# Patch embedding of a vision tower in nine full tiles of 128 patches, moved into attention tiles by transfers

## What is computed

```python
patches = _patchify(x, PATCH)                               # 32 x 36 x 768
tokens = jnp.einsum('bnd,ed->bne', patches, W) + b
out = jnp.concatenate([cls, tokens], axis=1)
h = out + pos_embedding
...
h = jnp.concatenate([jnp.broadcast_to(cls_tok, ...), h], axis=1)   # 32 x 38 x 256
h = h + _L0_attn_ref(_layernorm(h), ...)     # 1 + s + s*s/2, causal, divided by the row's sum
h = h + _L0_ffn_ref(_layernorm(h), ...)      # values and weights rounded to a 4-bit grid
h = h + _L1_attn_ref(_layernorm(h), ...)     # softmax, causal
h = h + _L1_ffn_ref(_layernorm(h), ...)      # gelu between low-rank products
```

## Time and profile before

| | |
|---|---|
| median of 3 runs | 257.46 us (257.4 to 257.49) |
| profiled execution | 258.99 us, its span 257.3 us |
| TensorE busy | 238.8 us (93%), 3077 records |
| VectorE busy | 183.2 us (71%) |
| ScalarE, GpSimd busy | 144.1 us (56%), 153.4 us (60%) |
| mean granted clock of TensorE | 0.996 |

### The profile page before, as it was taken

One profiled execution on the slowest core, in us unless ns is written; L12 is line 12 of the kernel. 1 busy time (PEld: TensorE's weight loads), 2 busy tenths in 40 slices (PEclk: granted clock), 3 DMA queues, 4 the chain that ended last, 5 costly groups with the idle time before them and its releaser, 6 DMA issues.

```text
span 257.3 us, 7730 instructions
## 1 busy us (share of the span) xinstructions
PE 238.8 (93%) x3077; PEld 187.0 (73%) x3077; DVE 183.2 (71%) x348; ACT 144.1 (56%) x322; POOL 153.4 (60%) x234
## 2 busy tenths in 40 slices
PE   6599999979999799999999998899999998989992
PEld 6488888858888687887887887688888885344331
DVE  0434968324679999999999999998768888377021
ACT  3122314287998677878746754574555556823640
POOL 6432888525966777795889749676656661155000
PEclk9999999999999999999999999999999999999998
DMA  5959942000000000000001010001101110001021
GB/s 149 242 135 248 302 103 65 0 0 4 3 3 3 0 3 3 3 0 4 4 20 36 25 40 29 20 30 40 35 28 34 33 35 33 3 0 54 19 75 48
DMA packets 12967, 12.26 MB, mean 48 GB/s; under 512 B 4464, under 2 KB 12356, under 8 KB 12932
## 3 DMA queue, kind: packets, MB, share of 16 engines
q1 hardware_dynamic: 12504, 11.76, 16.8%
q10 hardware_dynamic: 428, 0.01, 0.1%
HBM read 7.95 MB, written 1.25 MB: 36 GB/s over the span
## 4 chain that ended last, share of the span: by engine, by line
PE 61%; DVE 27%; issue 5%; DMA 3%; ACT 2%; SPq 0%; DVEq 0%; ACTq 0%
PE psum L1329 11%; PE psum L1398 9%; PE psum L1567 4%; DVE img L1092 4%; PE psum L1720 3%; DVE big L1084 3%; PE psum L1658 3%; DMA img<-in_x 3%; PE psum L1708 3%; PE psum L1552 3%; PE psum L1444 3%; DVE st L1039 3%; PE psum L1307 2%; PE psum L1632 2%; PE psum L1484 2%
## 5 line engine op out<-in xcount | busy, mean ns | idle before, releaser
L1398 PE MATMUL psum<-hnT,a 128*128 128x114 f32 (+1 forms) x352 | 48.5, 281 | 0.2 <-ACT mT L740 0.2
L1398 PEld LDWEIGHTS psum<-hnT,a 128*128 128x128 f32 x352 | 43.3, 191 | 4.8 <-issue 1.5
L486 POOL TENSOR_SCALAR big<-mT,parmask 128x228 f32<-128x228 f32 x22 | 22.8, 1048 | 19.8 <-ACT mT L710 19.8
L491 POOL TENSOR_SCALAR ve<-mvs 114x1 f32<-114x1 f32 x44 | 16.9, 384 | 28.0 <-DVE mvs L1041 25.8
L1329 PE MATMUL psum<-wT,patchT 128*114 128x256 f32 (+1 forms) x132 | 30.1, 381 | 0.4 <-ACT patchT L645 0.4
L492 POOL TENSOR_TENSOR rstd<-ve,nhalf 114x1 f32<-114x1 f32 x44 | 27.1, 615 | 3.7
L519 POOL TENSOR_TENSOR big<-big,img 114x912 f32<-114x912 f32 (+1 forms) x11 | 21.8, 1984 | 11.2 <-ACT big L775 11.0
L1329 PEld LDWEIGHTS psum<-wT,patchT 128*114 128x114 f32 (+1 forms) x132 | 22.5, 175 | 5.6 <-issue 0.9
L1084 DVE SCALAR_TENSOR_TENSOR big<-big,img 114x912 f32<-114x912 f32 (+1 forms) x11 | 16.5, 1498 | 8.9 <-ACT big L764 8.9
L764 ACT ACTIVATE big<-psum 114x912 f32<-114x912 f32 (+1 forms) x22 | 18.8, 906 | 6.0 <-PE psum L1444 5.8
L1039 DVE BATCH_NORM_STATS2 st<-h_all 114x6 f32<-114x256 f32 x44 | 18.8, 428 | 1.5
(11 more groups left out here) (169 smaller groups left out, 557.9 us busy)
## 6 DMA issues: line engine op xcount, KB each, us to landing
img<-in_x SPq DMA_DIRECT2D x6, 576.0 KB, 9.8
img<-v_tok SPq DMA_DIRECT2D x66, 38.0 KB
out<-h_all SPq DMA_DIRECT2D x10, 114.0 KB
w_raw<-in_L_tok_W SPq DMA_DIRECT2D x3, 256.0 KB, 7.8
a_raw<-in_L_attn_Wq SPq DMA_DIRECT2D x1, 256.0 KB, 6.8
a_raw<-in_L_attn_Wk SPq DMA_DIRECT2D x1, 256.0 KB, 7.0
a_raw<-in_L_attn_Wv SPq DMA_DIRECT2D x1, 256.0 KB, 7.2
a_raw<-in_L_attn_Wo SPq DMA_DIRECT2D x1, 256.0 KB, 9.9
```

The costliest lines, as they stand in the source:

```text
L486: nc.gpsimd.tensor_scalar(mX[:, :, o, :], mT[:, :, :], parmask[:, o:o + 1], None, ALU.mult).then_inc(L["mX"], 1)
L1398: return nc.tensor.matmul(bk[:, m * T:m * T + TW[t]], w[:, c, m * 128:(m + 1) * 128], hnT[:, c, 0:TW[t]], start=(c == 0), stop=(c == DC - 1))
```

## The change

The embedding no longer goes by attention tiles. The 1152 patches of all images are nine full tiles of 128 (`NE = 9`), without columns for the class rows, so `patchT` has 36 columns per image. VectorE copies an embedded tile as it is from PSUM into one of four places in `v_tok` (`stage(e)`, L1074 of the new kernel), which layer 1 uses later for its value rows. SP then carries the rows by image, 4 or 5 pieces per tile and 40 in all, from there to their partitions in `h_all` (L391), which starts out as zeros. The pieces stand on SP's queue behind `qw` and ahead of the weights of layer 1. When all pieces of an attention tile are there, `place(t)` adds `posb` in `h_all` and makes the statistics (L1080). Tiles 0 to 3 are placed before layer 0, tile 4 in turn 0 of its loop, 5 and 6 in turn 1, 7 to 10 in turn 2, each behind `divide`, and GpSimd's `rstd_embedded` follow them. GpSimd's memset of `v_tok` moves to turn 2. Staging e takes a place again only when tile e - 4 has been carried away.

On TensorE the order changes from the second half on: tiles 4 to 7 are embedded channel by channel between the transposes, and tile 8, instead of 9 and 10, inside `layer0`, two channels before the first key projection and one behind the transposes of the quantised weight. The first loads are issued in steps: the second image channel waits for the first weight piece, the third weight piece for the first image channel, and the second half's first channel for the second channel.

```diff
-        EB = [bank[n] for n in (4, 5, 6, 7, 4, 5, 6, 7, 4, 6, 6)]
-        EB_FREE = [0, 0, 0, 0, 1, 2, 3, 4, 5, 7, 10]
+        NP_IMG = G * G
+        NE = B * NP_IMG // 128
+        EB = [bank[n] for n in (4, 5, 6, 7, 5, 6, 7, 4, 6)]
+        EB_FREE = [0, 0, 0, 0, 2, 3, 4, 1, 6]
+        def pieces(e):
+            cuts = sorted({128 * e, 128 * (e + 1)} | set(range(-(-128 * e // NP_IMG) * NP_IMG, 128 * (e + 1), NP_IMG)))
+            return [(p // NP_IMG, p % NP_IMG, p - 128 * e, q - p) for p, q in zip(cuts, cuts[1:])]
...
             for c in range(CH):
+                if c == 2:
+                    sp.wait_ge(ld_img[0][0], 16)
                 sp.dma_start(w_raw[:, :, 2 * 128 * c:2 * 128 * (c + 1)], weights[:, :, 2 * 128 * c:2 * 128 * (c + 1)]
                              ).then_inc(ld_w[c], 16)
+                if c == 1:
+                    sp.wait_ge(ld_w[0], 16)
                 load_channel(0, c)
+            sp.wait_ge(ld_img[0][1], 16)
             load_channel(1, 0)
...
+            for e in range(NE):
+                sp.wait_ge(emb_sb, e + 1)
+                for b, first, at, n in pieces(e):
+                    row = b % TI * S + 2 + first
+                    sp.dma_start(h_all[row:row + n, b // TI, :], staged[at:at + n, e % 4, :]).then_inc(emb_moved[e], 16)
...
-            nc.gpsimd.memset(patchT[:, :, :, 0:2], 0.0).then_inc(consts, 1)
+            nc.gpsimd.memset(h_all[:, :, :], 0.0).then_inc(consts, 1)
...
-                    if t == 0:
-                        for u in range(EARLY + WIDE, NT):
-                            rstd_embedded(u)
+                    if t < 3:
+                        for u in ((4,), (5, 6), (7, 8, 9, 10))[t]:
+                            rstd_embedded(u)
                     if t == 2:
+                        nc.gpsimd.memset(v_tok[:, :, :], 0.0).then_inc(zeroed, 1)
...
-            def take_tile(t):
-                dve.wait_ge(emb_ps, t + 1)
-                nc.vector.tensor_tensor(h_all[:, t, :], EB[t][0:T, 0:D], posb[:, :], ALU.add
-                                        ).then_inc(emb_sb, 1)
-                dve.wait_ge(emb_sb, t + 1)
-                static_stats(t, var_ready)
+            def stage(e):
+                dve.wait_ge(emb_ps, e + 1)
+                if e >= 4:
+                    dve.wait_ge(emb_moved[e - 4], 16 * len(pieces(e - 4)))
+                nc.vector.tensor_copy(staged[:, e % 4, :], EB[e][:, 0:D]).then_inc(emb_sb, 1)
+            def place(t):
+                for e in parts_of(t):
+                    dve.wait_ge(emb_moved[e], 16 * len(pieces(e)))
+                nc.vector.tensor_tensor(h_all[:, t, :], h_all[:, t, :], posb[:, :], ALU.add).then_inc(placed, 1)
+                dve.wait_ge(placed, t + 1)
+                static_stats(t, var_e)
...
+            stage(0)
+            stage(1)
             take_chunk(KC)
+            stage(2)
+            stage(3)
             patches_of(1, 2)
             take_chunk(KC + 2)
+            place(0)
             take_chunk(KC + 4)
             weight_scales()
             weight_grid()
+            place(1)
+            for e in range(EARLY, EARLY + WIDE):
+                stage(e)
             weight_rounding()
             weight_values()
+            place(2)
+            stage(NE - 1)
+            place(3)
...
                     divide(t)
+                    if t < 3:
+                        for u in ((4,), (5, 6), (7, 8, 9, 10))[t]:
+                            place(u)
...
-                        last = nc.tensor.matmul(EB[t][0:TW[t], 0:D],
-                                                patchT[:, c, TI * t:TI * t + IMAGES[t], :].rearrange("p b s -> p (b s)"),
+                        last = nc.tensor.matmul(EB[t][:, 0:D],
+                                                patchT[:, c, :, :].rearrange("p b s -> p (b s)")[:, 128 * t:128 * (t + 1)],
                                                 wT[:, c, :], start=(c == 0), stop=(c == KC - 1))
```

More of the change, by code:

```diff
@@ L127, in vit_tower @@
         z = sb("z", [T, H])
-        v_tok = sb("v_tok", [T, 2, 2 * D])
+        v_tok_ = sb("v_tok", [128, 4 * D])
+        v_tok = v_tok_[0:T, :].rearrange("p (n d) -> p n d", n=2)
+        staged = v_tok_.rearrange("p (n d) -> p n d", n=4)
         oT = sb("oT", [128, DC, T])
@@ L183, in vit_tower, with parts_of @@
         OB = YB[:, D:D + DC * T]
-        EB = [bank[n] for n in (4, 5, 6, 7, 4, 5, 6, 7, 4, 6, 6)]
-        EB_FREE = [0, 0, 0, 0, 1, 2, 3, 4, 5, 7, 10]
+        NP_IMG = G * G
+        NE = B * NP_IMG // 128
+        EB = [bank[n] for n in (4, 5, 6, 7, 5, 6, 7, 4, 6)]
+        EB_FREE = [0, 0, 0, 0, 2, 3, 4, 1, 6]
         WIDE = 4
+        def pieces(e):
+            cuts = sorted({128 * e, 128 * (e + 1)} | set(range(-(-128 * e // NP_IMG) * NP_IMG, 128 * (e + 1), NP_IMG)))
+            return [(p // NP_IMG, p % NP_IMG, p - 128 * e, q - p) for p, q in zip(cuts, cuts[1:])]
+        def parts_of(t):
+            return range(TI * t * NP_IMG // 128, -(-(TI * t + IMAGES[t]) * NP_IMG // 128))
         KQ0 = bank[4]
@@ L213, in patch_slots @@
                 "p w (b g) -> p b g w", g=G)
-        EARLY = HALF // TI
+        EARLY = HALF * NP_IMG // 128
         def by_patch(eng, copy, half, c):
@@ L256, in vit_tower @@
         emb_sb = sem("emb_sb")
+        emb_moved = [sem(f"emb_moved{e}") for e in range(NE)]
+        placed = sem("placed")
+        var_e = sem("var_e")
         a0_ps = sem("a0_ps")
@@ L501, in rstd_embedded @@
             def rstd_embedded(t):
-                pool.wait_ge(var_ready, t + 1)
+                pool.wait_ge(var_e, t + 1)
                 step(static_rstd(t))
@@ L605, in _ @@
             bias_parts()
-            for t in range(EARLY):
-                rstd_embedded(t)
             pool.wait_ge(by_patch_dve, 4)
@@ L610, in _ @@
             nc.gpsimd.memset(pN, 0.0).then_inc(zeroed, 1)
-            nc.gpsimd.memset(v_tok[:, :, :], 0.0).then_inc(zeroed, 1)
             nc.gpsimd.memset(img1[:, H * KEYS:H * KEYS + 2 * TI * H * HD], 0.0).then_inc(zeroed, 1)
-            for t in range(EARLY, EARLY + WIDE):
+            for t in range(4):
                 rstd_embedded(t)
@@ L645, in _ @@
                 nc.scalar.activation(
-                    patchT[:, c, half * HALF:(half + 1) * HALF, 2:S].rearrange("p b (g w) -> p b g w", w=G),
+                    patchT[:, c, half * HALF:(half + 1) * HALF, :].rearrange("p b (g w) -> p b g w", w=G),
                     patch_slots(n), ACT.Copy).then_inc(img_act, 1)
@@ L994, in _ @@
             patches_of(0, 0)
-            dve.wait_ge(consts, 2)
             take_chunk(0)
@@ L1062, in _ @@
             weight_grid()
-            for t in range(EARLY, EARLY + WIDE):
-                take_tile(t)
+            place(1)
+            for e in range(EARLY, EARLY + WIDE):
+                stage(e)
             weight_rounding()
             weight_values()
-            for t in range(EARLY + WIDE, NT):
-                take_tile(t)
+            place(2)
+            stage(NE - 1)
+            place(3)
             dve.wait_ge(pool_step, POOL_STEPS)
@@ L1363, in _ @@
                 embed(t, [2])
-            embed(4, range(CH))
+            for t in (4, 5):
+                embed(t, [0])
             turn_channel(1, 1)
-            for t in range(EARLY, EARLY + WIDE):
-                embed(t, [0])
-            turn_channel(1, 2)
-            for channel in (1, 2):
-                for t in range(EARLY, EARLY + WIDE):
-                    embed(t, [channel])
+            for t in (6, 7):
+                embed(t, [0])
+            for t in (4, 5):
+                embed(t, [1])
+            turn_channel(1, 2)
+            for t in (6, 7):
+                embed(t, [1])
+            for t in range(EARLY, EARLY + WIDE):
+                embed(t, [2])
             def turn_quantised_weights():
-                pe.wait_ge(emb_sb, EARLY + WIDE - 1)
+                pe.wait_ge(emb_sb, EARLY + 3)
                 pe.wait_ge(wq_ready, 1)
@@ L1578, in layer0 @@
                     turn_weight(n)
-                embed(NT - 2, range(CH))
+                embed(NE - 1, range(CH - 1))
                 pe.wait_ge(a0_sb, 4)
@@ L1584, in layer0 @@
                 turn_quantised_weights()
-                embed(NT - 1, range(CH))
+                embed(NE - 1, [CH - 1])
                 q_proj0(0)
@@ L1592, in layer0 @@
                 turn0(2)
-                pe.wait_ge(emb_sb, NT)
+                pe.wait_ge(emb_sb, NE)
                 for t in range(NT):
```

13 lines of the change are left out of this document (4 added, 9 removed).

## The result

The changed kernel takes 263.47 us (median of 4 runs, 261.53 to 264.58) and the kernel before 257.43 beside it (4 runs, 257.31 to 257.49): a ratio of 1.0224, interval 1.0195 to 1.0254. The forecast was 258.4, the range 256.6 to 260.4. The direction was right, the size was not: +6.0 us where +0.9 was forecast. The profiled run of the changed kernel is the fastest of its four, 261.53 us with a span of 259.7; the other spans are 261.6 to 262.8, so the profile shows 4.1 of the 6 us, and the rest has to be found in the scatter. The ratios leave out a run that is over 1.5% slower than the fastest of its kernel, which happened once, with the last kernel but one.

What follows compares the result with a forecast made beforehand. It took TensorE's embedding chain to bound the start and VectorE, without idle time from about 73 us, layer 0. Span 257.3 - 3.4 + 4.3 = 258.2; on the median, 257.46 + 0.9 = 258.4 us, range 256.6 to 260.4.

Steps and rivals of the forecast that it cites:

- The placings: Layer 0: tiles 4 to 6 free, four placings in turn 2 delay VectorE; 4.3 us lost, bounds 3.5 and 5.3.
- the start: Everything before layer 0: fewer embedding matmuls make layer 0 start 3.4 us earlier, bounds 2.2 and 4.1.
- Step (1): Up to the second half's second-channel patch transposition: earlier first load worth nothing, gain 0.15 us; stepped loads take 0.4.
- The 0.4 for the steps: First loads: issuing them in steps delays the posb and tokb sum by 0.4 us, bounds 0 and +1.5.
- Step (2): From turn_channel(1, 1) to turn_channel(1, 2): work as before, one transposition and 16 records, 4.47 us.
- Step (3): From turn_channel(1, 2) to turn0(0): 6.6 us instead of 7.91, saving 1.3, less 0.3 for place(0) awaiting its rows.
- rival C: Before layer 0: pieces land late, place(0) and place(1) hold the chunk copy and turn0; 260.5 us, chance 0.09.
- Step (4): From turn0(0) to the end of the first query projection: 12 records instead of 24, 7.6 us for 10.19, saving 2.6.
- rival B: Layer 0: VectorE's mask and product separate from GpSimd's mask, returning 0.8 to 2 us; 257.5 with one, chance 0.2.
- rival D: Turn 3: TensorE idles nearly 4 us, its clock falls to half, adding 1 to 2 us; 260 us, chance 0.1.
- rival A: First loads: the queue clears earlier, tokb and images land about 2 us sooner, gain 5.6; 256.2 us, chance 0.13.
- a sum before 23.5: Start: the sum of posb and tokb, expected near 24.4 to 25; starting before 23.5 us would show the forecast wrong.

Runs made afterwards that it cites:

- the last kernel but one: Changed kernel with placings where VectorE idles, GpSimd's memsets later, its norm steps for tiles 7 to 10 one per turn; 253.28 us, ratio 0.9835, the fastest measured.
- the dummies: Kernel before plus four groups of add, statistics and aggregate on scratch data behind divide(2), shaped like placings; 262.61 us, ratio 1.0228.

## Why the prediction was wrong

Between the forecast of 258.4 and the measured 263.5 us lie 5.1. The step that failed most is the clock: the sum put it at nothing, and it costs 2.5 us. The placings cost 5.6 us and not 4.3, 1.3 more, and the start gained 2.4 and not 3.4, 1.0 less, both mostly by GpSimd's company, which the sum left out. 0.3 us stay without a place.

**The base.** The prediction carried the 1.53 us between the profiled run and the median through the sum unchanged. That holds only if the disturbance lies outside what the change moves. It lay in the first loads, and it made the start look later than it is. Against the recorded profile the start gained 52.29 - 48.43 = 3.86 us (scores of turn 0, 1 us behind the projection in the earlier trace rows), more than the 3.4 of the sum; against an ordinary run 2.4.

**Step (1)**, to the patch transposition of the second half: forecast -0.25 (0.15 less 0.4 for the steps); measured 27.12 to 26.69, a gain of 0.43. The 0.4 for the steps were seen in the sum of the tables (22.85 for 22.42) but in other runs not, 22.57 and 22.28; they were scatter. (The terms of this step add up to 28.5, not 28.6; it changes nothing.)

**Step (2)**, 4.47 as it was: right to the hundredth.

**Step (3)** is the first that failed. The way from 31.16 on was to be 6.6 us plus 0.3; it was 8.51. With late memsets it is 6.88, with the stagings in front as well 6.21, TensorE's own 6.2 of the forecast. The costs were counted instruction by instruction on VectorE, from rows in which nothing of GpSimd held VectorE. That GpSimd reaches its memsets at another time relative to VectorE was never asked. The feared landing of the pieces was no matter here: place(0) waited 2.18 us at 30.33 and ended ahead of the chunk copy (31.86), which waited for TensorE. So rival C, the late landing, did not come (its own terms give 257.46 - 1 + 4.3 = 260.8, not 260.5). A piece's issue took 0.73 us in the row of 17 (12.49 us), more than the 0.569 of the earlier trace rows, at no cost.

**Step (4)**, 2.6 us: right. 50.83 - 39.51 = 11.32 before, 48.43 - 39.67 = 8.76 after, 2.56.

**The placings** were the largest term, 4.3 us, bounds 3.5 and 5.3. Mechanism and place were right, and without company the size too: the dummies cost 4.7. In the changed kernel they cost 5.6, with turn 1's two that "cost nothing" (0.35) and an add of 1.81 us for 0.42. The same rows that priced rival B, masks of 1.85 us beside GpSimd, could have priced this: an added two-input instruction meets GpSimd's mask as well as the old ones do. Rival B looked at it only as a gain. In place of "4 x 1.02" stood 2.40 us for the first placing and 1.0 for each of the others, 5.4 in all.

**The clock**, rival D, was no rival but came on top. At a chance of 0.1 and 1 to 2 us it was both too unlikely and too small: a wait of nearly 4 us for TensorE was in the forecast's own case; 4.72 came, and the fall with it. The median carries 2.5 us, the larger part by all signs from the gap of 2.1 us of which the forecast knew nothing, because it came out of step (3).

Summed over the median: 257.4 - 2.4 (start) + 5.6 (placings) = 260.6, and the kernel with TensorE kept at work has 260.97; + 2.5 (clock) = 263.1 to 263.5. Of the signs that the prediction named, turn0(0) (39.67 for 39.9) and the scores (48.43 for 49) came out "right". That was luck: two errors had cancelled there, the late profile and the memsets. The sign of "wrong" that did come, a sum before 23.5, had been put down for rival A; in truth it was the ordinary start.

## What to carry to other kernels

Before the times of a profiled run go into a sum, ask where it is slower than the median, and don't carry the difference over as a constant. Where VectorE and GpSimd both work, price an instruction that is moved on one by what the other does at that moment, in both directions: a placing cost 1.0 us alone and 1.8 to 2.7 beside a mask, and of the 4.8 us that the best kernel was ahead at divide(0) 4.1 reached the end once most of the eleven placings stood where neither engine was in the way. And a forecast that makes TensorE wait several us has to price the slower clock: all four profiles here with a wait of 4.5 to 4.8 us had it.

## What the runs showed that I had not expected

- A VectorE instruction over 16 elements stood 1.80 us behind two GpSimd memsets of 0.94 and 1.37 us, and moving them was worth 3.3 us of the median: 1.65 of time, the rest by all signs of a clock that no longer fell there.
- TensorE's gap of 4.72 us dropped the clock in the profiled run, and it stayed at half into 89 us, over 4 us of full work. Gaps of 2.14, 2.17 and 2.24 us at one place of the program left it at 1.00, one of 2.28 dropped it to 0.50; a gap of 0.51 us left it at 1.00.
- The first loads land up to 1.5 us apart from run to run, with the same instructions up to there (kernel before and kernel with dummies). Over all kernels the first chunk's copy started at 9.01 to 9.25 us in eleven profiles, at 10.01 in one and at 10.71 in another.
